# Attention's result divided by its row sums in place and moved by DMA, without TensorE transposes; the negated maxima as 16-bit blocks ahead of a projection

## The reference, cut to what matters

```python
scores = jnp.einsum('bhsd,bhtd->bhst', query, key) * scale      # 16 heads, 64 + 64 wide
attn = jax.nn.softmax(scores, axis=-1)
out = jnp.einsum('bhst,bhtd->bhsd', attn, v)
x = x + ga * (out.reshape(B, S, H * VD) @ o_w.T)
# then layer norm, group-limited top 6 of 32 experts, their MLPs, a shared MLP, and a weighted sum
```

## Time and profile before

| | before |
|---|---|
| median of 3 runs | 2083.45 us (2078.28 to 2084.25) |
| the profiled execution | 2077.61 us |
| its span, first to last instruction | 2075.7 us |
| mean granted PE clock | 0.96 |
| attention's loop, in the span | about 160 to 1448 us |
| mixture up to the first routed tiles | about 1450 to 1686 us |

### The profile page before, as it was taken

One profiled execution on the slowest core, in us unless ns is written; L12 is line 12 of the kernel. 1 busy time (PEld: TensorE's weight loads), 2 busy tenths in 40 slices (PEclk: granted clock), 3 DMA queues, 4 the chain that ended last, 5 costly groups with the idle time before them and its releaser, 6 DMA issues. The chain is left out here.

```text
span 2075.7 us, 44742 instructions
## 1 busy us (share of the span) xinstructions
PE 1918.5 (92%) x14050; PEld 1015.4 (49%) x14050; DVE 1354.4 (65%) x2858; ACT 1389.4 (67%) x1924; POOL 1347.8 (65%) x804
## 2 busy tenths in 40 slices
PE   8969999999999999999999999998855499999996
PEld 6623444444444444444444444443733367777765
DVE  5867777777777877777777778771532245555553
ACT  5617888888888888888888888887520135555543
POOL 2327888888888888888888888888256313333330
PEclk9969999999999999999999999999977699999998
DMA  6179970000000000000000000000123429999988
GB/s 235 46 311 406 407 274 0 0 0 0 0 0 0 0 0 0 0 0 0 0 0 0 0 0 0 0 1 3 55 81 123 140 94 338 343 347 346 337 277 288
DMA packets 87873, 231.12 MB, mean 111 GB/s; under 512 B 12048, under 2 KB 45072, under 8 KB 87696
## 3 DMA queue, kind: packets, MB, share of 16 engines
q1 hardware_dynamic: 77072, 200.32, 27.0%
q0 software_dynamic: 10752, 30.16, 3.8%
HBM read 126.33 MB, written 104.10 MB: 111 GB/s over the span
## 5 line engine op out<-in xcount | busy, mean ns | idle before, releaser
L813 POOL TENSOR_TENSOR prob_lo<-prob,prob_hi 128x1024 f16<-128x1024 f32 x512 | 1085.1, 2141 | 246.8 <-ACT prob_hi L836 246.8
L885 DVE TENSOR_REDUCE maxes<-ring 128x1 f32<-128x512 f32 x1024 | 645.0, 683 | 195.4 <-PE ring L987 187.6
L834 ACT ACTIVATE prob<-p_s,prob_scale 128x1024 f32<-128x1024 f32 x512 | 570.3, 1114 | 262.1 <-PE p_s L1021 260.6
L836 ACT ACTIVATE prob_hi<-p_s,prob_scale 128x1024 f16<-128x1024 f32 x512 | 570.2, 1114 | 0.0
L987 PE MATMUL ring<-kr_hi,qr_hi 64*128 64x512 f16 x1024 | 379.6, 385 | 13.6 <-DVE qc_hi L872 7.4
L987 PE MATMUL ring<-kc_pair,qc_hi 64*128 64x512 f16 x1024 | 375.5, 384 | 0.0
L1289 POOL DMA_INDIRECT ranked_out<-y,dest x128 | 122.7, 959 | 268.6 <-DVE y L1591 265.4
L1021 PE MATMUL p_s<-qr_lo,kr_hi 64*128 64x512 f16 x1024 | 293.0, 377 | 0.0
L1021 PE MATMUL p_s<-qr_hi,kr_lo 64*128 64x512 f16 x1024 | 283.2, 377 | 0.0
L1021 PE MATMUL p_s<-qr_hi,kr_hi 64*128 64x512 f16 x1024 | 250.3, 382 | 1.6 <-ACT prob_hi L836 1.5
L1021 PE MATMUL p_s<-qc_lo,kc_one 33*128 33x512 f16 x1024 | 248.1, 379 | 0.0
(11 more groups left out here) (253 smaller groups left out, 2665.9 us busy)
## 6 DMA issues: line engine op xcount, KB each, us to landing
w<-in_experts SPq DMA_DIRECT2D x128, 608.0 KB
expert_rows<-zeros SPq DMA_DIRECT2D x129, 544.0 KB, 7.7
rows<-expert_rows SPq DMA_DIRECT2D x128, 136.0 KB
got<-ranked_out SPq DMA_DIRECT2D x16, 768.0 KB, 10.4
wqb<-in_wqb SPq DMA_DIRECT2D x8, 768.0 KB, 5.0
cbar<-in_woT SPq DMA_DIRECT2D x1, 2048.0 KB, 16.3
ranked_out<-y,dest POOLq DMA_INDIRECT x128
out<-x SPq DMA_DIRECT2D x16, 128.0 KB, 3.6
```

Source lines behind the costliest of these rows:

```text
L813: gp.tensor_tensor(prob_lo[s % NB][:, :], prob[s % 2][:, :], prob_hi[s % NB][:, :], ALU.subtract).then_inc(lo_ready, 1)
L834: act.activation(prob[s % 2][:, :], p_s[s % 2][:, :], ACT.Exp, bias=prob_scale[:, :], scale=SCALE / W_SCALE)
L836: act.activation(prob_hi[s % NB][:, :], p_s[s % 2][:, :], ACT.Exp, bias=prob_scale[:, :], scale=SCALE / W_SCALE).then_inc(p_ready, 1)
L885: v.tensor_reduce(maxes[:, at:at + 1], bank[:, :], AX.X, ALU.max).then_inc(ring_used, 1)
```

## The change

What it does:

- `turn` is gone from PE and DVE, and so are `turn_att` and `copy_turned`. `att_t` exists twice, and stays with the 2 x 33 rows on partitions. SP sends the two rows of sums to DRAM (2 DMAs), fetches them as 128 x 8 (1), DVE inverts them (`invert`, at the start of group 2), SP sends them to DRAM (1) and fetches them spread over 32 partitions each as `recip_wide` (2). DVE multiplies (`scale`, ahead of group 7), and SP moves the two blocks of 32 rows into `cbar` (2), which now has tokens along the free axis, so that `project` reads it directly.
- The 129 clears are issued five at a time behind these DMAs, in 26 half-heads.
- One DMA chain is left at attention's end; its steps stand in mixture, with `invert` after tile 2 and `scale` after tile 4, and `project` waits for it before tile 8.
- `maxneg` holds 16-bit blocks 64 wide: the reduction goes to `maxraw`, and a second instruction scales it by -1/1024 into `maxneg`. `rows` stands after the last round of group 6, directly ahead of `rest`, and is 16-bit.
- The place of `turn` in the order of the ring goes to a `pause` behind the first use: that use counts twice, and its bank's neighbour is left out.

The diff, cut to its core:

```diff
-            sp.dma_start(wkz[:, :], a["wk"]).then_inc(ld_wk, 16)
+            sp.dma_start(wkz[:, :], a["wk"]).then_inc(ld_ov, 16)
...
+def send_sums(sp, k, scaling, done):
+    for c in range(2):
+        sp.dma_start(sums_dram[k:k + 1, c * QC:(c + 1) * QC],
+                     att_t[k % 2][c * CP + C:c * CP + C + 1, :]).then_inc(done, 16)
+def fetch_sums(sp, k, scaling, done):
+    sp.dma_start(sums[:, :], sums_dram[k:k + 1, :].rearrange("o (p j) -> (o p) j", p=P)).then_inc(done, 16)
+def send_recips(sp, k, scaling, done):
+    sp.dma_start(recips_dram[k:k + 1, :].rearrange("o (p j) -> (o p) j", p=P), sums[:, :]).then_inc(done, 16)
+def spread_recips(sp, k, scaling, done):
+    for c in range(2):
+        sp.dma_start(recip_wide[k % 2][c * CP:c * CP + C, :],
+                     recips_dram[k:k + 1, c * QC:(c + 1) * QC].to_broadcast([C, QC])).then_inc(done, 16)
+def store_heads(sp, k, scaling, cbar, done):
+    h, half = k // 2, k % 2
+    for c in range(2):
+        at = h // 4 * S + half * 2 * QC + c * QC
+        sp.dma_start(cbar[h % 4 * C:(h % 4 + 1) * C, at:at + QC],
+                     att_t[k % 2][c * CP:c * CP + C, :]).then_inc(done, 16)
...
-        maxneg = sb("maxneg", 4 * KR, F32R)
-        att_t = sb("att_t", QC)
+        maxraw = sb("maxraw", 8)
+        maxneg = sb("maxneg", 4 * CP, F16)
...
-                aside = {(1, 0): ("turn", not first), (6, 8): ("rows", more)}.get((g, len(rounds)))
+            if more and g == 6:
+                rounds.append([("rows", None, None, None)])
             if after and g in (5, 6):
                 rounds.append([({5: "rope", 6: "rest"}[g], None, None, None)])
...
+        EVENTS.insert(1, "pause")
...
+            for k in range(2 * H - 1):
+                sp.wait_ge(o_copied, k + 2)
+                send_sums(sp, k, scaling, moved)
+                sp.wait_ge(moved, MOVES * k + 32)
+                fetch_sums(sp, k, scaling, moved)
+                if k:
+                    sp.wait_ge(stored, 32 * k)
+                    sp.sem_inc(freed, 1)
+                sp.wait_ge(answered, 2 * k + 1)
+                send_recips(sp, k, scaling, moved)
+                sp.wait_ge(moved, MOVES * k + 64)
+                spread_recips(sp, k, scaling, moved)
+                clear(min(5 * k, BLANKS), min(5 * k + 5, BLANKS))
+                sp.wait_ge(answered, 2 * k + 2)
+                store_heads(sp, k, scaling, cbar, stored)
...
                     if s == 3 and more:
-                        act.wait_ge(ring_mm, use_of(2 * h, "turn")[0] + 1)
                         copy_wq(h + 1)
...
                 if last:
                     v.wait_ge(ring_used, use + 1 + RING)
-                    v.tensor_reduce(maxneg[:, :].rearrange("p (j z) -> p j z", j=4)[:, :, 0:KR:C], by_tile, AX.X, ALU.max,
-                                    negate=True).then_inc(neg_ready, 1)
+                    pairs = maxraw[:, :].rearrange("p (j c) -> p j c", j=4)
+                    step(v.tensor_reduce(pairs, by_tile, AX.X, ALU.max))
+                    v.tensor_scalar(maxneg[:, :].rearrange("p (j z) -> p j z", j=4)[:, :, 0:KR:C], pairs, -1.0 / MAX_SCALE, None,
+                                    ALU.mult).then_inc(neg_ready, 1)
                     v.wait_ge(neg_ready, m + 1)
             def rows(m, half, use, bank):
...
-                step.mark(v.tensor_scalar(qc_lo[half][C:C + 1, :], bank[0:1, :], 1.0 / MAX_SCALE, None, ALU.mult))
+                step.mark(v.tensor_copy(qc_lo[half][C:C + 1, :], bank[0:1, :]))
...
-            def turn(half, h, use, bank):
...
+            def invert(m):
+                v.wait_ge(moved, MOVES * m + 48)
+                v.reciprocal(sums[:, :], sums[:, :]).then_inc(answered, 1)
+            def scale(m, half):
+                v.wait_ge(moved, MOVES * m + MOVES)
+                v.wait_ge(o_copied, m + 2)
+                v.tensor_tensor(att_t[half][0:CP + C, :], att_t[half][0:CP + C, :], recip_wide[half][0:CP + C, :],
+                                ALU.mult).then_inc(answered, 1)
...
                 for g in range(len(MAX_AT)):
-                    for now in plan(g, first, more, after):
+                    if g == 2 and not first:
+                        invert(m - 1)
+                    if g == len(MAX_AT) - 1 and not first:
+                        scale(m - 1, 1 - half)
+                    for now in plan(g, more, after):
...
                 for j in range(4):
-                    last = pe.matmul(bank[0:KR, j * P:(j + 1) * P], maxneg[:, j * KR:(j + 1) * KR], identr[:, :],
+                    last = pe.matmul(bank[0:CP, j * P:(j + 1) * P], maxneg[:, j * CP:(j + 1) * CP], ident16[:, :],
                                      start=True, stop=True)
...
             def project(t):
-                pe.wait_ge(ct_ready, t + 1)
+                if t == T // 2:
+                    pe.wait_ge(stored, 64 * H)
+                if t == 0:
+                    pe.wait_ge(col_ready, 1)
                 if t >= 2:
                     pe.wait_ge(x_used, t - 1)
                 for g in range(4):
-                    last = pe.matmul(p_y[t % 2][:, 0:D], ctb[t % 2][:, g * P:(g + 1) * P], wov[:, g * D:(g + 1) * D],
+                    last = pe.matmul(p_y[t % 2][:, 0:D], cbar[:, g * S + t * P:g * S + (t + 1) * P], wov[:, g * D:(g + 1) * D],
                                      start=(g == 0), stop=(g == 3))
```

More of the change, by code:

```diff
@@ L770, in attention, with uses_of @@
         MAXIMA = [(c, n) for g in range(len(MAX_AT)) for now in plan(g) for what, c, n, part in now if what == "max" and part == 1]
+        EVENTS.insert(1, "pause")
         USES = len(EVENTS)
+        assert USES % RING == 0
+        def uses_of(what, first):
+            return 2 if what == EVENTS[0] and not first else 1
         def use_of(m, what, first=False, more=True, after=True):
             place = EVENTS.index(what)
-            if first and place < EVENTS.index("turn"):
+            if first and place < EVENTS.index("pause"):
                 place += 1
@@ L951, in _ @@
             half_head(H - 1, 1, more=False, after=False)
-            copy_out(2 * H - 1)
-            turn(1, H - 1, use_of(2 * H - 1, "turn", more=False)[0] + 1, ring[-1 % RING])
+            copy_out(2 * H - 1, 1)
         @block.tensor
         def _(pe):
-            for s, n in ((ring_used, RING), (p_ready, 2), (lo_ready, 2), (o_mm, NB), (o_copied, 1)):
+            for s, n in ((ring_used, RING), (p_ready, 2), (lo_ready, 2), (o_mm, NB), (o_copied, 1),
+                         (freed, 2)):
                 pe.sem_inc(s, n)
@@ L976, in project_rest, with maximum @@
                 project(1, half, use, bank)
-            def maximum(c, n, part, m, half, use, bank):
+            def maximum(c, n, part, m, half, use, bank, uses=1):
                 j, kc = n // 4, n % 4
@@ L1049, in half_head @@
                             elif what == "max":
-                                maximum(c, n, part, m + 1, 1 - half, *use_of(m, (c, n), *state))
-                            elif what == "turn":
-                                turn(m - 1, *use_of(m, "turn", *state))
+                                maximum(c, n, part, m + 1, 1 - half, *use_of(m, (c, n), *state), uses_of((c, n), first))
                             elif what == "rows":
@@ L1313, in _ @@
             act.wait_ge(col_ready, 1)
-            for t in range(2):
-                copy_turned(t)
             act.wait_ge(pads, 1)
@@ L1681, in _ @@
             last.then_inc(col_mm, 1)
-            for t in range(2):
-                turn_att(t)
-            pe.wait_ge(col_ready, 1)
             for t in range(T + 3):
```

138 lines of the change are left out of this document (70 added, 68 removed).

## The result

The changed kernel takes 2191.1 us (median of 4 runs, 2188.9 to 2193.4), 1.052 times the kernel before (interval 1.050 to 1.054): 108 us slower, where 86 were forecast, and 3 above the range. Its profiled span is 2191.3 against 2075.7, +115.6; the two profiled executions lie on opposite sides of their medians.

What follows compares the result with a forecast made beforehand. DVE's chain from the last maximum to the copy was taken as the bound: +3.0 a half-head over thirty half-heads gave +90, mixture -4.5, total +86, so 2168 us. The range was 2108 to 2188.

Steps and rivals of the forecast that it cites:

- What bounds the kernel: Attention's loop: DVE's chain from the last maximum to the copy binds; what is put into it lands on the time.
- The wait for POOL: DVE instructions with SBUF sources wait until POOL's running operation ends; the small TENSOR_SCALAR too, making rope +1.53 later.
- The chain: DVE, last maximum to copy: rope +1.53, its sum +2.98, copy +3.3 or +3.7, mean +3.5 a half-head.
- PE's part: PE per half-head: turn saves 0.59, 16-bit rows at most 0.2, the pause costs 0.215.
- The sum per half-head: Attention's loop: 3.5 + 0.2 - 0.6 = +3.1, with half of rows' saving +3.0; thirty half-heads, +90.
- the gap in which PE idles is not won back: groups 0 to 6 are PE's own pace: PE in each half-head behind the copy: the delay stays in full, so thirty half-heads give +90.
- Ahead of the first copy: First half-head, which has no scale: left out of the thirty with the full chain, no cost counted, 0.
- Mixture: After attention: final turn gone -1.9, two turn_att gone -1.9, tiles -1.6, invert and scale +0.9; sum -4.5.
- DMAs: Eight per half-head, in a chain of four steps through the loop: all hidden, 0.
- the first (only scale waits, 2118): DVE's chain: the small TENSOR_SCALAR slips through, only scale waits for POOL; +35, 2118; chance 0.20.
- a late DMA chain: Loop: invert or the second copy_out waits for DMAs, 1 to 2 a half-head on top; 2195 to 2225; chance 0.03.
- a chain that doesn't bind: Loop: scale falls into POOL's gaps and PE's freed time counts in full; -28, 2055; chance 0.04.

Runs made afterwards that it cites:

- the kernel before with one instruction more: Kernel before, maxima reduced into a scratch tile and negated by a second instruction, a TENSOR_SCALAR of 4 x 2 elements: 2127.6 us (before 2078.3).
- the pause moved: Changed kernel with maxima negated in one instruction, scale ahead of group 5, and the pause behind the seventh use, in group 1: 2057.0 us, ratio 0.9898.
- the fillers: Changed kernel plus nine matmuls a half-head, results unread, just ahead of the pair of maxima for which PE waits: 2167.8 us, ratio 1.0417.
- the fastest version: Changed kernel with one-instruction negated maxima, scale ahead of group 5 and the pause behind the seventh use: 2057.0 us, ratio 0.9898 to the kernel before.
- the kernel with the one-instruction maxima: Changed kernel, maxima negated by one TENSOR_REDUCE into bfloat16 maxneg, 1/1024 in the two copies of rows, scale still ahead of group 7: 2135.4 us.
- the kernel before with the extra product: Kernel before plus a DVE multiplication of two 97 x 512 SBUF tiles ahead of group 7, result unread, no DMA added: 2193.9 us.

## Why the prediction was wrong, step by step

- **What bounds the kernel**: right. A delay of DVE's chain appears in full in the time (the chain of the kernel before with one instruction more: +39 in the loop), and a part of DVE's 23% idle time is worthless for it.
- **The wait for POOL**: right, the tiny TENSOR_SCALAR included (0.18 with POOL at rest, 1.84 in the loop).
- **The chain**: right. It has to be counted from the reduction of the maxima in both kernels, since the TENSOR_SCALAR that writes `maxneg` starts 0.22 behind it. From there to `rope` it is 2.19 against 0.64, +1.55 (forecast 1.53); to the end of the sum +2.98, as forecast; to the copy 14.97 and 14.91 against 11.69 and 11.32, +3.28 and +3.59 (forecast 3.3 and 3.7), mean 3.4 (forecast 3.5). These are medians over 26 half-heads.
- **PE's part**: right. Turn and pause together should give -0.4. From the copy to the reduction it was 28.91 in the kernel before and is 28.53 in the changed kernel's half-heads at full clock, -0.38; with the pause moved it is 28.32, -0.59, the turn alone, to the hundredth.
- **The sum per half-head**, +3.0: 43.45 at full clock less 40.42 is 3.03. There are 29 half-heads with the full chain and not 30 (the distance between the thirtieth copy and the next is 38.4 in both kernels), so it is 88 where 90 were forecast.
- **The step that failed is the one that said "the gap in which PE idles is not won back: groups 0 to 6 are PE's own pace"**, with that pace taken as the one of the kernel before. The forecast busy share of 93% (91% measured) is some 3 us of idling in each half-head, but I had the clock only in what the trace of before showed, 1.00, where there was no idling of that kind. What the runs showed in its place: behind the copy PE ran at 1.2 GHz for some 3 us, which costs 1.7 us in 15 of 29 half-heads, +25. Without it the profiled span would be +90 and inside the range; with the fillers, which remove nearly all of it, the kernel is at 2167.8, beside the forecast's 2168. That it agrees to the unit is luck: the fillers' kernel is 2.4 later at the first copy, 92 longer in the 29 half-heads and 3.5 shorter behind the last copy than the kernel before.
- **Ahead of the first copy**: taken as 0, measured +3.6. The first half-head has no scale, but it has the TENSOR_SCALAR and the late sum like all the others, and the copy follows the chain: 12.55 from reduction to copy against 11.13, +1.4, which should have been counted. The other 2.1 lie ahead of that reduction, which starts between 189.6 and 193.1 in the kernels run here, and between 189.6 and 192.6 in three whose code is the same up to there; they stay open.
- **Mixture**: -4.5 forecast, -2.0 at the end. At the twelfth tile's addition the changed kernel was 6.2 ahead (37.3 behind its last copy against 43.5); it gave 4 back later. The same stretch took 622.7 to 627.7 in the six other kernels with this code, so a difference of 2.5 between forecast and result can't be judged.
- **DMAs**: right, 0. `invert` shows no idle time ahead of it in the loop (3.0 once, behind the thirty-first copy, where there are no maxima), and the fastest version has them all.
- **The rivals**: the first (only scale waits, 2118) is nearly the kernel with the one-instruction maxima; it measured 2135, and again the clock is the difference (1.64 in 12 half-heads, 20 us). Neither a late DMA chain nor a chain that doesn't bind was seen.

## What to carry to other kernels

Before putting an instruction into an engine's idle time, find the chain that the others wait for, and put it outside: the same multiplication cost 1.6 to 2.0 us in the chain (and 1.7 more where the clock fell), 0.4 in one group and nothing that shows in another. When a forecast makes PE idle where it did not before, add a rival in which the clock falls behind it, priced from any row at the lower level. A tiny DVE instruction between tiles of SBUF can cost the rest of the POOL operation beside it and not its own time: the TENSOR_SCALAR here did (1.84), the reductions into `maxneg` did not (0.19). And look for the reverse too: POOL waits as well, and whoever waits for POOL.

## What had not been expected of the hardware

- PE's granted clock fell after idle stretches of 2.06 to 2.61 us in the kernel before with the extra product (behind all 29 copies that had one), and after 2.26 to 2.35 us in the changed kernel (15 times in 29 distances, the idle times alike in all). With scale in group 4 there were 1.60 us of idling in every half-head and it stayed up; with the fillers it fell once behind 1.63. It lasted some 3 us, seven steps at 0.43. What else than the length of the idling decides it was not tried.
- A TENSOR_SCALAR over eight elements waited for the running POOL operation in every half-head, 1.84 to 1.86 each time, as forecast from a single row of the program's start; a reduction from SBUF to SBUF just ahead of it, beside the same operation, did not wait (0.19 each time).
- A DVE instruction of 0.68 with two sources in SBUF that started 0.01 to 0.02 ahead of a POOL operation made POOL's pair last 4.74 and not 4.22.
